# Feed-forward rows of three groups: scaled by GpSimd in channel order, sent through DRAM as blocks, turned by VectorE instead of TensorE

## The reference, cut to what matters

```
x = x + ffn(layernorm(x))
h = round(x @ w1 + b1, 2**-8)
h = piecewise-linear gelu of h, 33 points on [-4, 4], rounded to 2**-8
out = round(h @ w2 + b2, 2**-8)
```

## Time and profile before

| | |
|---|---|
| median of 3 runs | 1586.78 us (1586.59 to 1586.93) |
| profiled execution, its own time | 1586.93 us |
| its span, first to last instruction | 1585.0 us |
| granted TensorE clock, mean | 0.999 of full speed |
| busy over the span | PE 99%, weight loads 87%, DVE 79%, ACT 64%, POOL 52% |

### The profile page before, as it was taken

The page is one execution under the profiler, slowest core; times in us unless marked ns, Lnnn a source line. Parts: engine busy times, 40 slices in busy tenths (PEclk is TensorE's granted clock), DMA queues, the critical chain, the costliest instruction groups (busy, mean ns, idle before and its releaser), DMA issues. The chain is left out here.

```text
span 1585.0 us, 30386 instructions
## 1 busy us (share of the span) xinstructions
PE 1569.8 (99%) x11114; PEld 1377.5 (87%) x11114; DVE 1245.0 (79%) x2409; ACT 1021.1 (64%) x2025; POOL 822.0 (52%) x784
## 2 busy tenths in 40 slices
PE   9999999999999999999999999999999999999998
PEld 7889899898999989999899888988988887888886
DVE  6558878887888878878788685767777889989887
ACT  3457777777777777777787442445446666666765
POOL 3318657376573856747456242333334555555554
PEclk9999999999999999999999999999999999999999
DMA  8984636456364654635433684432436601011010
GB/s 253 271 258 150 180 111 189 127 169 176 117 185 120 178 164 128 187 108 152 139 112 95 186 284 137 136 90 81 139 96 222 244 14 61 20 36 39 7 54 27
DMA packets 203412, 215.60 MB, mean 136 GB/s; under 512 B 83776, under 2 KB 149632, under 8 KB 203264
## 3 DMA queue, kind: packets, MB, share of 16 engines
q1 hardware_dynamic: 203264, 213.66, 43.8%
HBM read 154.88 MB, written 58.72 MB: 135 GB/s over the span
## 5 line engine op out<-in xcount | busy, mean ns | idle before, releaser
L79 PE MATMUL p_bank_score<-p_ctxt,p_qo 128*128 128x256 f32 x2304 | 304.6, 286 | 0.8 <-ACT p_probs L1112 0.4
L79 PEld LDWEIGHTS p_bank_score<-p_ctxt,p_qo 128*128 128x128 f32 x2304 | 288.1, 191 | 5.9 <-issue 2.2
L79 PE MATMUL p_bank_mix<-p_probt,p_ctx 128*128 128x512 f32 x1152 | 292.0, 397 | 0.5
L79 PEld LDWEIGHTS p_bank_mix<-p_probt,p_ctx 128*128 128x128 f32 x1152 | 207.4, 189 | 41.8 <-issue 3.8
L1316 DVE SCALAR_TENSOR_TENSOR p_qo<-p_bank_mix,p_odd,p_qo 128x512 fp32r<-128x512 f32 x192 | 143.8, 749 | 57.6 <-ACT p_qo L1126 50.1
L1126 ACT ACTIVATE p_qo<-p_bank_mix,p_odd 128x512 fp32r<-128x512 f32 x192 | 132.4, 690 | 68.2 <-PE p_bank_mix L79 67.6
L1112 ACT ACTIVATE p_probs<-p_bank_score,p_small 128x257 f32<-128x257 f32 x256 | 121.5, 475 | 58.6 <-DVE p_small L1297 54.1
L801 POOL TENSOR_SCALAR p_probs<-p_probs,p_small 128x256 f32<-128x256 f32 x256 | 122.2, 485 | 68.9 <-DVE p_small L1303 68.8
L795 POOL TENSOR_TENSOR p_ctx<-p_ctx_in,p_ctx 128x768 fp32r<-128x768 f32 x64 | 118.5, 1851 | 66.7 <-ACT p_ctx L1101 66.4
L790 POOL TENSOR_TENSOR p_ctx_in<-p_ctx_in,p_odd_in 128x768 f32<-128x768 f32 x64 | 118.2, 1847 | 40.2 <-DMA p_odd_in<-in_ctx_dram 40.2
L1297 DVE TENSOR_REDUCE p_small<-p_bank_score 128x1 f32<-128x257 f32 x256 | 105.4, 415 | 10.2 <-PE p_bank_score L79 7.6
(11 more groups left out here) (302 smaller groups left out, 3917.4 us busy)
## 6 DMA issues: line engine op xcount, KB each, us to landing
p_blocks_in<-in_ctx_dram SPq DMA_DIRECT2D x256, 96.0 KB, 2.4
p_ctx_in<-in_ctx_dram SPq DMA_DIRECT2D x64, 384.0 KB, 3.1
q<-p_ctx SPq DMA_DIRECT2D x64, 256.0 KB, 3.7
ffn<-p_w_raw SPq DMA_DIRECT2D x64, 256.0 KB, 2.9
p_odd_in<-in_ctx_dram SPq DMA_DIRECT2D x64, 192.0 KB, 3.6
p_x<-in_x_dram SPq DMA_DIRECT2D x32, 256.0 KB, 4.1
p_quad<-q SPq DMA_DIRECT2D x32, 256.0 KB, 3.6
p_probt<-q SPq DMA_DIRECT2D x32, 256.0 KB, 3.8
```

The lines of the kernel that those rows point to most:

```text
L79: made = e.matmul(out, lhsT, rhs, start=n == 0, stop=n == last)
```

## The change

For tiles 4 to 15, POOL now scales (`scale_ordered`). It reads a row of 512 floats with a stride of 4 floats in its innermost dimension (`a j k` walked as `a k j`) and writes it contiguously into `sums`, a buffer that the output sums also use. SP writes that to DRAM (`put_row`) and reads it back in four DMAs of 32x32 blocks into `p_x` (`load_blocks`). DVE then turns the blocks by one STREAM_TRANSPOSE into the PSUM bank (`turn_blocks`) where it scaled before, at the step where PE turned. PE's transposes are gone.

```diff
@@ sync, per step n
+                for i in tile_at(n, SCALED):
+                    put_row("n", i)
+                    load_blocks("n", i)
@@ gpsimd
+            def scale_ordered(i):
+                x_is_in(e, "z", i)
+                if i == after.early:
+                    e.wait_ge(after.norm.steps, 14)
+                if i >= 2 * NRF:
+                    e.wait_ge(out_done, NRF * (i // NRF - 1))
+                if i >= after.early + 2:
+                    e.wait_ge(n_put, DMA * (i - 1))
+                made = x_of("z", i).rearrange("p (a j k) -> p a k j", k=KT, j=QUAD)
+                e.tensor_scalar(sums[i % 2][:].rearrange("p (a k j) -> p a k j", k=KT, j=QUAD), made,
+                                after.norm.minus[:, i:i + 1], after.norm.inv[:, i:i + 1], ALU.add,
+                                ALU.mult).then_inc(after.norm.chain, 1)
...
             for n in range(1, NF):
+                for i in tile_at(n, SCALED):
+                    scale_ordered(i)
                 rest_by_slope(n)
@@ tensor
-                for i in tile_at(n, TURNED):
-                    after.norm.turn(e, i)
@@ vector
-                for i in tile_at(n, SCALED):
-                    scaled_rows(i)
+                for i in tile_at(n, TURNED):
+                    e.wait_ge(n_blocks[i % 2], NB * DMA * (i // 2 + 1))
+                    after.norm.turn_blocks(e, i, ordered=True)
                 snap(n)
                 for i in tile_at(n, TURNED):
                     after.norm.low(e, i, zts_next[(g + 1) % 2], i % NRF * P)
```

More of the change, by code:

```diff
@@ L174, in turn, with turn_blocks @@
         made.then_inc(self.turned, 1)
-    def turn_blocks(self, e, i):
+    def turn_blocks(self, e, i, ordered=False):
         bank, z = self.bank(i), self.home(i)
@@ L182, in turn_blocks @@
             e.wait_ge(self.lo, self.last_in_bank(i) + 1)
-        e.transpose(bank.rearrange("p (k a r) -> p a k r", k=C // P, r=QUAD),
-                    z.rearrange("p (a j k) -> p a k j", k=C // P, j=QUAD)).then_inc(self.turned, 1)
+        blocks = z.rearrange("p (a k j) -> p a k j" if ordered else "p (a j k) -> p a k j", k=C // P, j=QUAD)
+        e.transpose(bank.rearrange("p (k a r) -> p a k r", k=C // P, r=QUAD), blocks).then_inc(self.turned, 1)
     def high(self, e, i, zt, row):
@@ L1711, in put_row @@
                 e.wait_ge(scaled.chain, i + 1)
-                e.dma_start(z_dram[at, i], scaled.home(i)).then_inc(done, DMA)
+                rows = sums[i % 2][:] if kind == "n" and i >= after.early else scaled.home(i)
+                e.dma_start(z_dram[at, i], rows).then_inc(done, DMA)
             def load_blocks(kind, i):
@@ L2212, in low_h @@
                                            op1=ALU.subtract).then_inc(h_lo, 1)
-            def scaled_rows(i):
-                x_is_in(e, "z", i)
-                after.norm.scale(e, i, x_of("z", i))
             def down_sum(i):
```

## The result

| | before | changed |
|---|---|---|
| median of six executions, us | 1586.78 (1586.59 to 1586.93) | 1599.34 (1599.25 to 1599.41) |
| span of the profiled execution, us | 1585.0 | 1597.5 |
| granted TensorE clock, mean | 0.999 | 0.999 |

The change makes the kernel slower: the ratio is 1.0079, with a 95% interval of 1.0066 to 1.0092, and the difference 12.56 us. The clock is the same, so it has no part in this.

A forecast was written before the change was run, and what follows sets the result against it. PE and DVE's element loop run at nearly one pace, so the loop sets the price: 5.0 + 4.6 + 4.6 = +14.2 us on 1586.78 gives 1601.0. Likeliest range 1597 to 1603; over all cases 1583 to 1603.5.

The forecast's parts named there:

- PE's 5.6 us: PE's four transposes cost 0.47 us a tile; removing them for twelve tiles gains 5.6 us at most.
- turn step: DVE loop step that scales and turns, three a group: next `round_up` at 8.23 instead of 6.86, 1.37 us later.
- step 29: Loop step that turns without scaling: taken as +0.1 us, from 0 to +0.4.
- X: Length of POOL's strided scaling, not in the trace: bounds 0.77 and 1.28 us, middle 1.03 taken.
- flat stretch: For X from 0.89 to about 2, a step that scales and turns loses the same 1.37 us.
- first scaling: Step 21 of a group, scaling without a turn: two steps take 11.27 instead of 10.21 us, +1.06.
- 1.1 more: Case within the range: 1.1 us more at each group's first scaling if `join` loses there too.
- The first group: Loop loses 0.8 + 4.1 + 0.1 = 5.0 us; PE pays all of it, since it waited already.
- The slack: The loop comes 0.7 us ahead of PE in each later group, so PE pays 5.3 - 0.7 there.
- rival of late blocks: DVE stands at the transpose 1 us a tile, up to 12 us: about 1599 without the collision; chance 0.02.
- Faster: POOL's scaling finds the way free or lets `rest` pass and is short: -4.1 us, 1582.7; chance 0.24.
- Half the burden: Scaling asks before `step`, +8.2 us, 1595.0; or X under 0.89, +3.1, 1589.9; half or less, chance 0.30.

The follow-up runs named there:

- pool_alone: One part of the change alone, POOL scaling with the 16-byte stride; no DRAM trip or DVE turn, PE keeps its transposes: 1599.37 us.
- the pair on ACT: Scaling moved to ACT, once in the changed kernel (1582.64 us), once in the kernel before, where PE still turns (1586.07 us).
- behind_rest: Changed kernel with one wait more: POOL's scaling waits until DVE's `rest` of the same step is done: 1590.80 us.
- short_scale: Changed kernel, but POOL scales only the first three quarters of each row, all of it for tiles 4 and 5: 1596.77 us.
- contiguous_scale: Changed kernel, but POOL reads the row contiguously and DVE's transpose does the reordering: 1588.59 us.
- act_scale: Changed kernel, but ACT scales in channel order behind `ends` instead of POOL; one small DVE instruction makes the offsets: 1582.64 us.
- contiguous_behind_rest: Changed kernel with POOL's scaling contiguous, DVE's transpose reordering, and the scaling waiting for DVE's `rest`: 1585.32 us.

## Why the prediction was right, step by step

The forecast was 1601.0 us, the time 1599.34: +12.6 in place of +14.2. The mechanism was the right one: POOL's scaling goes ahead of `rest`, `join` then loses to the difference and the product, and PE waits for the loop. The signs that the prediction named for step 23 were there with other sizes: `rest` lengthened by 0.96 and not 0.7, the two `join` by 0.49 and 0.86 and not 1. The terms behind the sum were off as follows.

- **The loop is to be priced, not PE.** Shown. pool_alone and the whole change take the same time with 5.6 us of PE's work between them.
- **PE's 5.6 us.** Right in size, as the pair on ACT bears out (3.4 us of gain and 1.9 of new waits), and hidden in the changed kernel.
- **The transpose was mis-sized.** I took 1.08 us from a row that reads with the reordering in it; the new one reads contiguously and took 0.71. So ACT's `high`, `ends` and POOL's difference came 0.39 earlier (the difference at 4.49 after `round_up` and not 4.88), and with them the end of the chain of holds. `step` gained less than 0.1 of this, since it waited for POOL's product until about 2.68. The turn step grew by 0.99 and not by 1.37, and step 29 by nothing and not 0.1. That it is not held by POOL was right: 711 to 715 ns in all twelve.
- **The scaling on DVE was never 1.31 us of DVE's work.** It takes 0.55, and the rest was its own wait for POOL's product, for which `step` waits now. So its going brings the next `round_up` forward by 0.34 only (6.86 against the 6.52 of step 29), and the transpose in its place, which does not wait for POOL, costs nothing: pool_alone has the same 7.85 with no transpose on DVE at all. The schedule of the prediction came out right here, because it took the places of the rows and not their lengths.
- **X, the scaling's length, was mis-sized.** It is 1.29 us, at the upper bound that I gave, not 1.03. Some 0.04 of it seems to be a wait for `step`: in behind_rest, where no `step` is in its way, it took 1.25 to 1.28 at the turn steps. At the turn steps this changed nothing, as the flat stretch said and short_scale showed. The edge of that stretch at 0.89 was worked out with the difference at 4.88; `join` came at 5.18 with a scaling of 1.31 and at 4.94 with one of 1.07, so with the difference at 4.49 an estimate of the edge is 0.6. At the first scaling it did: `join` asks at 4.56 us after `round_up`, just behind the difference at 4.47, and loses there too. This is the case that the range had as "1.1 more". The three rows of DVE at step 21 show it:

```profile
1341.87 1.64 DVE L2208 SCALAR_TENSOR_TENSOR p_rest<-p_v,p_rest 128x512 f16<-128x512 bf16 x1
1343.44 1.78 DVE L2219 SCALAR_TENSOR_TENSOR p_pieces_q<-p_pieces_q 128x512 f32<-128x512 f32 x1
1345.25 1.54 DVE L2222 SCALAR_TENSOR_TENSOR p_m<-p_m,p_pieces_q 128x512 f32<-128x512 f32 x1
```

  The first scaling cost 2.23 and not 1.06. With the scaling at 1.07 us in short_scale it cost 6.64 + 4.61, against 6.66 + 4.61 in the forecast.
- **The first group** came out at 3.1 and not 5.0. Its three turn steps lost about 1.0 each like the others; its first scaling lost 0.15 and not 0.8. POOL's timeline there, and DVE's behind it, show what my schedule left out:

```profile
1248.73 2.33 POOL L1856 TENSOR_SCALAR p_sum<-p_x,p5a_ln_minus,p5a_ln_inv 128x512 f32<-128x512 f32 x1 [0.83 <-DVE p5a_ln_inv L145]
...
1248.79 0.69 DVE L2208 SCALAR_TENSOR_TENSOR p_rest<-p_v,p_rest 128x512 f16<-128x512 bf16 x1
1249.40 0.68 DVE L2219 SCALAR_TENSOR_TENSOR p_pieces_q<-p_pieces_q 128x512 f32<-128x512 f32 x1
1250.12 1.48 DVE L2222 SCALAR_TENSOR_TENSOR p_m<-p_m,p_pieces_q 128x512 f32<-128x512 f32 x1
```

  The scaling waits for the statistics, comes when DVE already runs its two-input instructions without a gap, and is itself the one that queues (2.33 us). Only the second `join` is held. By my order of the queues the scaling should have gone in ahead of the first `join`; here it let that one pass as well. It is not a chance of one execution: the same scaling took 2.31 us in pool_alone and in short_scale, and 1.84 in contiguous_scale, with `rest` and the first `join` passing each time. Why was not tried, and stays open.
- **The slack** that the loop had (0.7 twice) gave back 0.8 and not 1.4: after group three the changed loop is 13.3 us behind, and the span is 12.5 longer. By its terms the sum is 3.1 + 5.2 + 5.2 - 0.8 = 12.7, less the 0.2 that the changed loop was ahead at the start. The closeness of the sum is partly luck, since the errors went both ways: the nine turn steps made it 3.4 too high and the first scalings of groups two and three 2.3 too low.
- **PE's idle time** was forecast at some 20 us, and the rows have 14.8. From the spans it must be 12.5 + 5.6 = 18.1 more than the 1.2 of before. The other 4.5 us stand in no row of waits; that they lie inside the busy time, since the ends of matmuls are modelled, is a guess.
- **The blocks** were in time in each of the twelve; the rival of late blocks did not come up. From the end of the scaling to the transpose the changed kernel leaves 7.1 us in the first scaling of group one, and 10.05 to 10.08 in the eleven others. In act_scale 6.2 us were enough there without a wait, and at step 23, where issuing the four block reads took 2.88 us in place of 1.75, the transpose waited 0.29 us and stood 6.6 us behind. So an estimate of what there was to spare is 0.5 to 0.9 us in group one and some 3.5 elsewhere; I had said 2.
- **The rivals.** "Faster" needed `rest` to get in first. behind_rest forced that, and it was still slower than before at 1590.8, since with X at 1.29 `join` loses instead. Only with the contiguous scaling as well did the time fall to that of before and 1.5 us under it (1585.3). "Half the burden" needed the scaling to come ahead of `step`, which it did at none of the twelve.

For access, the trace shows who holds whom, whole instruction by whole instruction. This is what the Trainium skill (SBUF — State Buffer, Who interferes with whom) states of the pair that DVE and POOL share, and act_scale agrees with it from the other side, since the second `join` kept 0.69 us beside ACT's 1.30. On X the Trainium skill was nearer than my choice: from its 2.9 cycles an element for a read with a stride (GPSIMD Engine Reference, Performance pitfalls for Q7 kernels) the estimate was 1.2 us, and the traces have 1.29 with the stride and 0.84 without, or 1.25 and 0.77 where the scaling waited for nobody (behind_rest and contiguous_behind_rest, at the turn steps).

## What to carry to other kernels

Where two engines run at nearly one pace, price an edit on the loop that sets the waits, not on the engine with the highest busy share: here 5.6 us less for an engine at 99% and the same 5.6 us kept gave one and the same time. Work moved to GpSimd beside VectorE instructions with two SBUF inputs costs by the moment at which it asks and by who waits behind it. Its length counts where it decides who gets in first, and hardly elsewhere: one more wait gained 8.5 us; a scaling of 1.07 us in place of 1.29 gained 2.6, nearly all at the first scalings; one of 0.84, with a transpose 0.39 longer on VectorE, let `join` in first and gained 10.8. Try ScalarE before GpSimd for such work, since it held up nobody here.

## What the runs showed of the hardware

- A VectorE transpose in 32x32 blocks of 128x512 f32 from SBUF to PSUM took 0.71 us with a contiguous read, and 1.05 to 1.12 with 16 bytes between elements; it kept its length beside POOL's product (0.71 in the changed kernel, 1.10 in contiguous_scale).
- GpSimd's scaling of 128x512 f32 took 1.29 us with that stride and 0.81 to 0.85 without; 128x384 took 1.07. Where no DVE instruction held it up the two took 1.25 and 0.77. ScalarE's took 1.30 and 0.80. VectorE's, contiguous, took 0.55 alone and 1.39 behind POOL's product.
- GpSimd, once it waits for the access, goes ahead of VectorE's next instruction, even where VectorE's own queue runs without a gap; the one exception seen is the first scaling of group one, above, in each of the four kernels in which it asked beside `rest`. With the hold times that the prediction read off the kernel before (DVE 0.57 us, POOL to 0.14 before its recorded end), the steps of groups two and three in the experiments could be worked out ahead to within some 0.05 us, once the lengths of the scaling and the transpose were measured: 7.05 expected and 7.01 measured for contiguous_scale, 7.2 and 7.20 to 7.24 for behind_rest, 6.75 and 6.76 for both together.
